# Graph network on one core: 16 instead of 18 of 28 columns on TensorE, and the ten candidates of a column side by side

## What is computed

```
x = layernorm(x + segment_sum(tanh(x[src] * edge_weight), dst))
x = layernorm(x + attention(x, edge_attr, src, dst))
x = layernorm(x + segment_max(x[src] * edge_weight1, dst) @ W.T + b)
x = layernorm(x + log_softmax(two GIN convolutions: segment_sum(x[src], dst), two dense layers each))
```

## Time and profile before

| | us |
|---|---|
| median of 3 runs | 8114.27 (8110.42 to 8117.8) |
| profiled execution, first to last instruction (span) | 8106.3 |
| TensorE matmuls busy in the span | 7107.4 (88%) |
| VectorE busy | 6896.2 (85%) |
| GpSimd busy | 5221.6 (64%) |
| ScalarE busy | 2239.6 (28%) |

### The profile page before, as it was taken

How to read it: one execution, slowest core, us unless ns; L and a number is a source line. 1 busy time by engine, 2 the same in 40 slices (tenths; PEclk the granted TensorE clock), 3 DMA queues, 4 the chain that set the end, 5 groups by cost and what they waited for, 6 DMA issues and landing times.

```text
span 8106.3 us, 209725 instructions
## 1 busy us (share of the span) xinstructions
PE 7107.4 (88%) x77871; PEld 6661.2 (82%) x77871; DVE 6896.2 (85%) x12224; ACT 2239.6 (28%) x7389; POOL 5221.6 (64%) x4570
## 2 busy tenths in 40 slices
PE   5999985999999999999995399998599996899994
PEld 5999984777777787777774399998599996899994
DVE  7999985999999999999997688888588885788884
ACT  0000003666666666666664100000000000000000
POOL 3555557888888888888886555555555555455554
PEclk9999997999999999999997699999799998899997
DMA  2223222555555555555554211111111111111110
GB/s 84 85 87 88 84 56 81 159 158 159 159 160 160 160 160 160 159 158 158 159 160 134 65 49 46 48 49 40 36 49 45 49 49 28 43 49 49 49 45 22
DMA packets 738222, 757.28 MB, mean 93 GB/s; under 512 B 153760, under 2 KB 698336, under 8 KB 738112
## 3 DMA queue, kind: packets, MB, share of 16 engines
q1 hardware_dynamic: 592640, 667.34, 24.9%
q0 software_dynamic: 140528, 86.77, 7.1%
q10 hardware_dynamic: 5008, 2.59, 0.1%
HBM read 239.80 MB, written 519.73 MB: 94 GB/s over the span
## 4 chain that ended last, share of the span: by engine, by line
PE 42%; DVE 29%; issue 23%; POOL 4%; DMA 1%; DVEq 1%; ACT 0%; ACTq 0%; another core or an unknown queue 0%; POOLq 0%; SPq 0%
PE ps L823 42%; DVE amax_room L1232 7%; DVE spare L1237 4%; DVE flat L1259 3%; DVE flat L954 2%; POOL got L456 2%; DVE msg L1137 2%; DVE stt L954 2%; DVE spare L1241 1%; DVE run L1158 1%; DVE wide_buf L954 1%; DVE raw L954 1%; POOL wide_buf L456 1%; DVE junk L1164 1%; DVE wide_buf L1116 1%
## 5 line engine op out<-in xcount | busy, mean ns | idle before, releaser
L456 POOL DMA_INDIRECT msg<-feat,cidx x1680 | 1681.5, 1001 | 1594.4 <-PE ps L823 1109.8
L823 PE MATMUL ps<-parts,wide_buf 128*128 128x160 bf16 x30240 | 2128.9, 233 | 289.0 <-DVE wide_buf L1116 276.4
L823 PEld LDWEIGHTS ps<-parts,wide_buf 128*128 128x128 bf16 x30240 | 2102.5, 98 | 304.8 <-issue 288.2
L456 POOL DMA_INDIRECT hsrc<-feat,aidx x1568 | 1921.5, 1225 | 461.1 <-issue 445.5
L823 PE MATMUL ps<-parts,flat 128*128 128x160 bf16 x30240 | 2118.5, 233 | 29.7 <-DVE flat L1116 16.7
L823 PEld LDWEIGHTS ps<-parts,flat 128*128 128x128 bf16 x30240 | 2093.3, 98 | 43.1 <-DVE flat L1116 21.4
L870 PEld LDWEIGHTS ps<-wsb,zT 102*128 102x128 f32 x9408 | 1462.9, 190 | 217.8 <-ACT zT L690 196.3
L870 PE MATMUL ps<-wsb,zT 102*128 102x192 f32 (+1 forms) x9408 | 1539.8, 313 | 99.0 <-ACT zT L690 98.5
L954 DVE TENSOR_TENSOR raw<-ps,amask 128x960 f32<-128x960 f32 x448 | 738.4, 1657 | 468.1 <-PE ps L823 286.5
L1137 DVE TENSOR_REDUCE msg<-raw 128x288 f32<-128x2880 f32 x224 | 1129.9, 5044 | 7.7
L657 ACT ACTIVATE cidx<-sidx 128x10 int32 (+1 forms) x224 | 46.8, 211 | 3684.6 <-DMA msg<-feat,cidx 3065.6
(11 more groups left out here) (220 smaller groups left out, 5229.9 us busy)
## 6 DMA issues: line engine op xcount, KB each, us to landing
state_tab<-flat SPq DMA_DIRECT2D x784, 512.0 KB
raw<-quot_tab SPq DMA_DIRECT2D x224, 576.0 KB
run_tab<-run SPq DMA_DIRECT2D x224, 224.0 KB
top_tab<-spare SPq DMA_DIRECT2D x392, 128.0 KB
msg<-feat,cidx POOLq DMA_INDIRECT x1680
hsrc<-feat,aidx POOLq DMA_INDIRECT x1568
efs<-in_ef SPq DMA_DIRECT2D x392, 34.0 KB
msg<-in_x,cidx POOLq DMA_INDIRECT x560
```

What stands on the lines that cost most here:

```text
L456: return pool.indirect_dma_start(dest, None, table, rows_at(idx))
L823: last = nc.tensor.matmul(block.rearrange("p (q c) -> p q c", c=D), hot[s][:, m, t * P:(t + 1) * P], parts[:, m * Q:(m + 1) * Q, part, :], ...
```

## The change

R goes from 18 to 16, so A from 10 to 12: in each group 240 matmuls instead of 270, one-hots of 2048 instead of 2304 columns, and 12 gathers. TensorE gives 12 marks in a group. The list that SP loads has 16 columns. The ten shared columns take three full banks (9 columns) and one of the last (1 column), which VectorE reads in two instructions; the one for the last bank comes first and has a semaphore of its own, `s_rest`, for which TensorE waits too. `parts` is laid out as [block, part, feature, candidate], so that a column's result in PSUM, `picked` and the mask have the ten candidates of a feature side by side; the sum over them reads neighbours. `split` first lays the features out in that order in `left` (three steps: memset, copy, copy) and then makes the parts. `wide_buf` and `flat` have 7168 instead of 8064 words.

```diff
-R = 18
+R = 16
...
-        parts = sb("parts", [P, MB * Q, 3, D], BF)
+        parts = sb("parts", [P, MB, 3, D, Q], BF)
...
-        picked = raw[:, R * P:R * P + R * QW].rearrange("p (r q c) -> p r q c", q=Q, c=D)
+        picked = raw[:, R * P:R * P + R * QW].rearrange("p (r c q) -> p r c q", q=Q, c=D)
...
                         if t == OWN and not (first and s == 0):
+                            pe.wait_ge(s_rest, n * NG + 2 * j + s)
                             pe.wait_ge(s_share, n * NG + 2 * j + s)
...
                                 last = nc.tensor.matmul(
-                                    block.rearrange("p (q c) -> p q c", c=D),
-                                    hot[s][:, m, t * P:(t + 1) * P], parts[:, m * Q:(m + 1) * Q, part, :],
+                                    block.rearrange("p (c q) -> p c q", q=Q),
+                                    hot[s][:, m, t * P:(t + 1) * P], parts[:, m, part],
...
-                link(v.tensor_copy(parts[:, 0:NB, 0, :], features[:]))
-                link(tt(nt[:], features[:], parts[:, 0:NB, 0, :], ALU.subtract))
-                link(v.tensor_copy(parts[:, 0:NB, 1, :], nt[:]))
-                link(tt(nt[:], nt[:], parts[:, 0:NB, 1, :], ALU.subtract))
-                v.tensor_copy(parts[:, 0:NB, 2, :], nt[:]).then_inc(s_parts, 1)
+                left = junk[:, 0:MB * QW].rearrange("p (m c q) -> p m c q", c=D, q=Q)
+                whole = NB // Q
+                link(v.memset(left[:, whole], 0.0))
+                link(v.tensor_copy(left[:, 0:whole], features[:, 0:whole * Q].rearrange("p (m q) c -> p m c q", q=Q)))
+                link(v.tensor_copy(left[:, whole, :, 0:NB - whole * Q], features[:, whole * Q:NB].rearrange("p q c -> p c q")))
+                link(v.tensor_copy(parts[:, :, 0], left))
+                link(tt(left, left, parts[:, :, 0], ALU.subtract))
+                link(v.tensor_copy(parts[:, :, 1], left))
+                link(tt(left, left, parts[:, :, 1], ALU.subtract))
+                v.tensor_copy(parts[:, :, 2], left).then_inc(s_parts, 1)
...
                     dve.wait_ge(q["pick"][s], (done + j + 1) * A)
-                    tt(picked_rows(OWN, R), shared.rearrange("p b (r c) -> p b r c", c=D), mask_rows(OWN, R),
-                       ALU.mult).then_inc(s_share, 1)
+                    tt(picked[:, R - LAST:R], shared[:, (R - OWN) // CB, 0:LAST * QW], mask_rows(R - LAST, R), ALU.mult).then_inc(s_rest, 1)
+                    tt(picked[:, OWN:R - LAST], shared[:, 0:(R - OWN) // CB], mask_rows(OWN, R - LAST), ALU.mult).then_inc(s_share, 1)
+                    dve.wait_ge(s_rest, n * NG + 2 * j + s + 1)
...
-                    hold(v.tensor_reduce(msg[:, s, A:U, :], picked.rearrange("p r q c -> p r c q"), AX.X, ALU.add))
+                    hold(v.tensor_reduce(msg[:, s, A:U, :], picked, AX.X, ALU.add))
```

More of the change, by code:

```diff
@@ L58 @@
 OI = 14
+BANKS = OWN // CB
+LAST = (R - OWN) % CB
+WIDE = 4 * DC * DD
+assert MB * R * P // 2 <= WIDE and 4 * K <= WIDE and NS * P <= WIDE
 assert NB % 2 == 1 and SL < NG // 2 and NB % DC == 0 and K % (2 * G) == 0 and NG % 2 == 0 and 2 * G == 8
 CONT, BOTH, CONT_NEG, BOTH_NEG = range(4)
-assert MB * (Q - 1) < NB <= MB * Q and CB * QW <= 512 and OWN == 2 * CB and R - OWN == 4 * CB and K % DW == 0
+assert MB * (Q - 1) < NB <= MB * Q and CB * QW <= 512 and OWN % CB == 0 and 2 * OWN // CB + -(-(R - OWN) // CB) <= 8 and K % DW == 0
 FP = mybir.dt.float32
@@ L167, in gnn_program @@
         raw = sb("raw", [P, R * P + R * QW])
-        wide_buf = sb("wide_buf", [P, 7 * R * P // 2])
+        wide_buf = sb("wide_buf", [P, WIDE])
         amax_room = sb("amax_room", [P, 2 * DC * DD])
@@ L176, in gnn_program @@
         wts = z_room[:, 0:K]
-        flat = sb("flat", [P, 7 * R * P // 2])
+        flat = sb("flat", [P, WIDE])
         st = flat[:, 0:2 * G * TW].rearrange("p (a g c) -> p a g c", a=2, g=G)
@@ L224, in gnn_program @@
         msgs = [ps[:, s * G:(s + 1) * G, DD:2 * DD] for s in range(2)]
-        mine_banks = [ps[:, 2 * s:2 * s + 2, 0:CB * QW] for s in range(2)]
-        shared = ps[:, 4:8, 0:CB * QW]
+        mine_banks = [ps[:, BANKS * s:BANKS * (s + 1), 0:CB * QW] for s in range(2)]
+        shared = ps[:, 2 * BANKS:8, 0:CB * QW]
         s_list = sem("s_list")
@@ L285, in gnn_program @@
         s_share = sem("s_share")
+        s_rest = sem("s_rest")
         NARROW = ("idx", "quot", "hot", "pick", "read", "got", "mul", "act", "run", "put")
@@ L586, in _ @@
             pool.memset(ones[:], 1.0).then_inc(s_zero, 1)
-            pool.memset(parts[:, NB:MB * Q], 0.0).then_inc(s_zero, 1)
             pool.iota(nidi[:, 0:NS], [[1, NS]], base=-1, channel_multiplier=NB).then_inc(s_iota, 1)
@@ L838, in _ @@
             pe.wait_ge(s_const, 16 * 9)
-            pe.wait_ge(s_zero, 4)
+            pe.wait_ge(s_zero, 3)
             pe.wait_ge(s_part, 1)
@@ L1122, in pick @@
                             count[:, MB:MB + Q].unsqueeze(1).to_broadcast([P, R, Q]), ALU.is_equal))
[L1123 to L1124 removed]
                     def mask_rows(lo, hi):
[L1127 removed]
+                        return amask[:, lo:hi, :].unsqueeze(2).to_broadcast([P, hi - lo, D, Q])
                     dve.wait_ge(q["pick"][s], (done + j) * A + OWN * A // R + 1)
[L1130 to L1131 removed]
+                    tt(picked[:, 0:OWN], mine_banks[s], mask_rows(0, OWN), ALU.mult).then_inc(q["read"][s], 1)
                     dve.wait_ge(q["pick"][s], (done + j + 1) * A)
[L1133 to L1134 removed]
+                    tt(picked[:, R - LAST:R], shared[:, (R - OWN) // CB, 0:LAST * QW], mask_rows(R - LAST, R), ALU.mult).then_inc(s_rest, 1)
+                    tt(picked[:, OWN:R - LAST], shared[:, 0:(R - OWN) // CB], mask_rows(OWN, R - LAST), ALU.mult).then_inc(s_share, 1)
+                    dve.wait_ge(s_rest, n * NG + 2 * j + s + 1)
                     dve.wait_ge(s_share, n * NG + 2 * j + s + 1)
                     dve.wait_ge(q["read"][s], done + j + 1)
[L1137 removed]
+                    hold(v.tensor_reduce(msg[:, s, A:U, :], picked, AX.X, ALU.add))
                 def round_(j, more, first, slice_=False, next_=False):
```

5 lines of the change are left out of this document (removed).

## The result

The changed kernel takes 8476.94 us (median of 4 runs, 8471.22 to 8501.29) where the kernel before takes 8113.88 in the same comparison (4 runs): ratio 1.0454, 95% interval 1.0439 to 1.0469. The prediction of 7619 us, faster with 0.97, was wrong by 858 us and in the sign.

The account below looks back on a forecast made before the run. TensorE was taken to bound passes 1 to 3 and VectorE pass 0. Savings of 352 + 12.5 + 128.5 + 9 + 1 - 7.6 = 495 us from a span of 8106.3 gave 7611, or 7619 us as median; range 7580 to 7675.

Parts of the forecast that it names:

- What bounds the kernel: Narrow passes: TensorE bounds passes 1 to 3 (18.85 us a group), VectorE pass 0 (19.87 a slice group), GpSimd third.
- Matmuls: TensorE's narrow passes: 30 fewer of 270 a group save 117.3 us in each of passes 1 to 3, 352 together.
- The cover: Narrow groups: VectorE's round and GpSimd's gathers (15.85 us in plain groups) stay hidden under TensorE's 16.76 us.
- Pass 0: Its 50 slice groups: 13 gathers end to end set 17.3 us for 19.87, a gain of 128.5 us.
- The sum: VectorE's sum over ten candidates: reading neighbours takes 2.82 us a group, 2.22 less than before.
- The new wait of TensorE: After 90 matmuls of a group TensorE waits for two reads of the shared banks instead of one: costs nothing.
- Once in each pass: Pass ends and starts, four passes: shared products and sum save 9 us, first one-hots 1, the longer split costs 7.6.
- The rival on the slower side: Chance 0.02: every wait for a mark costs GpSimd 1.5 us, passes 1 to 3 lose 563 us, time 8870 us.
- The other rival on gathers: Chance 0.06: gathers and one-hots exclude each other, so passes 1 to 3 gain only 84 us, time about 8015 us.
- The chances: Odds for the whole kernel: faster by over 0.2% 0.97, same 0.01, slower 0.02.
- the first case: GpSimd near 17.3 us a slice group in pass 0: 7605 to 7675 us, chance 0.62.
- What would show it: Signs of error: gathers' mean over 1.1 us, sum above 4 us, or TensorE waiting for one-hots in passes 1 to 3.

Follow-up runs that it names:

- the run with half the gathers: Changed kernel with every second gather of the narrow passes replaced by a GpSimd memset of 930 elements, odd rows zero: 7634.05 us, one run.

## Why the prediction was wrong, step by step

- *What bounds the kernel*: right for VectorE in pass 0 and TensorE in passes 1 to 3, but incomplete. That GpSimd with 13 us of work in 18.85 "comes third" was read from its busy time. The gathers have a second price, on TensorE, which 10 in 18.85 us, spread by marks, just escape.
- *Matmuls*, 117.3 us a pass: right as far as TensorE is left alone. With half of the gathers gone passes 1 to 3 take 931 to 932 us (forecast 938 to 940), 69.4 ns a matmul.
- *The cover*, and this is the step that failed: "The cover must hold: VectorE's round and GpSimd's gathers have to stay below 16.76". I tested it with GpSimd's own time, 12 x 1.245 + 0.9 = 15.85 us, and charged TensorE nothing. Shown: 12 gathers in a group of 16.76 us hold TensorE's stream back to 20.38 us. That is 608 us in passes 1 to 3 and 251 in pass 0, 859 together.
- *Pass 0*, 128.5 us gained by 13 gathers end to end in 17.3 us: the same error in its purest form, since end to end is what hurts. Of its 251 us some 41 may be VectorE's (1006.4 us in the run with half the gathers, for 966).
- *The sum*: 2.82 us forecast, 2820 ns measured; the products 1.16, 0.33 and 1.66 forecast, 1158, 325 and 1648 ns. Five one-hots take 3.41 us in a row like that of 3.74 before, so 0.33 less, as forecast; their mean with all that stands beside them fell from 819 to 751 ns each.
- *The new wait of TensorE*: nothing forecast (the reads were to end 3.6 us after the start; the terms given add up to 3.45), none seen: of its idle time in the narrow passes 1626.5 us are ended by issue and 266.4 by the one-hots at the starts of passes, none by a read of the banks.
- *Once in each pass*: from the last matmul of pass 1 to the first of pass 2 it is 108.5 us for 108.1, from pass 2 to pass 3 112.7 for 113.0. Forecast was 0.6 less a pass; the shorter sum and the longer split cancel within 1 us.
- *The rival on the slower side* had the right engine and the wrong mechanism. Waits cost nothing; their absence does. I dismissed it with "A GpSimd that is late finds its marks set and catches up", and the catching up is the damage. The other rival on gathers had them held back by one-hots; they were held back no more than before (977 ns on average, 1001 before).
- *The chances*: 0.97 on faster left no room for a cost outside my list. The upper end of the first case, 7675, is also 11 us above what its own terms give (7619 + 35 + 10 = 7664), which changes nothing here.
- *What would show it*: I named waits of TensorE for one-hots, which didn't come; I hadn't thought of waits for nothing.

What is shown: the loss needs GpSimd's gathers (not equal transfers from ScalarE, not a busy GpSimd), doesn't depend on their rows, is set off by their closeness alone (the kernel before without its waits), comes where four starts lie within some 4.5 us, and begins at the eleventh or twelfth gather of a run in place of the fourth when TensorE has a third of the instructions and weight loads. About an eighth of it is the lower clock that goes with the stops. What is only argued: that it is the supply of TensorE's instructions which the gathers hold up. No version beat the kernel before: 18 columns with the new layout are the same within 0.2%, 17 are 1% slower, since what a column less saves (1.05 us a group) is under what a gather more costs there (1.4).

## What to carry to other kernels

An engine's work can cost another engine time without a semaphore, a queue or a tile between them, so check a cover not only by "does it fit into the time" but by "what does the covering engine do while this runs": put the two engines' rows of the trace side by side once, at the densest place. Where a stream of small TensorE instructions runs beside indirect gathers, look at the densest place and not at the average (here four gathers in more than 4.75 us were all but free, four in under 4.25 us cost TensorE 1 us each time), and keep waits that spread them: a wait that looks like slack can be what protects the bound. When an engine's idle time is ended by "issue" in the middle of a stream, look for what else happened at that moment before trusting any sum of durations.

## What the runs showed of the hardware that I hadn't expected

- Gathers issued by GpSimd 1.25 us apart leave TensorE one to five matmuls of 160 columns every 0.71 us, mostly from the fourth gather on; with matmuls of 480 columns it is one at a time, from the eleventh or twelfth on. Four starts within 4.25 us cost 1.02 us, over 4.75 us 0.04 (13 traces).
- The stops fall before a matmul as often as before a weight load (706 and 703 times in the changed kernel), and no instruction packet is moved by DMA from 4800 to 5800 us, where they go on.
- A gather of 64 partitions takes 954 ns and one of 128 takes 977, and they disturb alike.
- Matmuls over 64 of the 128 rows ran all narrow passes at a granted clock of 0.50, 133 ns each, with TensorE busy throughout; those over 128 rows had 1.00 in passes 1 to 3 of the kernel before and 0.97 to 0.99 in the changed one.
